# Edge counts and weight sums of a graph: blocks of 10 destinations in one PSUM bank, and each chunk's one-hots made once

## The reference

```python
N, C, E = (50000, 256, 9375)
msg = ew[:, None] * h[src]
agg = jax.ops.segment_sum(msg, dst, num_segments=x.shape[0])
```

```python
dst = jnp.concatenate([_d, _s, _loop])
_o = jnp.argsort(dst, stable=True)
dst = dst[_o]
```

## Time and profile before

| | us |
|---|---|
| median of three runs | 5758.88 |
| lowest and highest run | 5757.93, 5769.3 |
| span of the profiled execution | 5765.0 |
| of it `count_edges`: first to last instruction of its engines | 791.5 to 1649.2 |

### The profile page before, as it was taken

One profiled execution on the slowest core, in us unless ns is written; L12 is line 12 of the kernel. 1 busy time (PEld: TensorE's weight loads), 2 busy tenths in 40 slices (PEclk: granted clock), 3 DMA queues, 4 the chain that ended last, 5 costly groups with the idle time before them and its releaser, 6 DMA issues. The chain is left out here.

```text
span 5765.0 us, 88635 instructions
## 1 busy us (share of the span) xinstructions
PE 4607.2 (80%) x24482; PEld 3873.4 (67%) x24483; DVE 2716.3 (47%) x5068; ACT 2120.2 (37%) x3279; POOL 836.5 (15%) x769
## 2 busy tenths in 40 slices
PE   3888868888856499669589989899769959969666
PEld 2677645555545399438578778788659959969555
DVE  5555567777653400321379689689631140020233
ACT  2333215544433200424256566566524420020332
POOL 2778710000005200002100000000022200000000
PEclk8788889999968799789799999999779979989878
DMA  3433311211113342113211111111122134224000
GB/s 97 113 111 106 101 37 71 79 71 75 66 62 100 106 161 109 30 34 116 65 51 56 46 44 55 42 49 55 39 71 97 36 93 162 109 92 159 36 17 24
DMA packets 150165, 438.52 MB, mean 76 GB/s; under 512 B 25592, under 2 KB 89805, under 8 KB 133676
## 3 DMA queue, kind: packets, MB, share of 16 engines
q1 hardware_dynamic: 115212, 341.23, 16.7%
q0 software_dynamic: 34848, 96.08, 5.9%
HBM read 340.98 MB, written 96.25 MB: 76 GB/s over the span
## 5 line engine op out<-in xcount | busy, mean ns | idle before, releaser
L2404 PE MATMUL p_acc<-p_H,p_eT 125*125 125x256 f32 x3750 | 823.5, 378 | 0.0
L2404 PEld LDWEIGHTS p_acc<-p_H,p_eT 125*125 125x125 f32 x3750 | 695.2, 187 | 106.0
L1033 POOL DMA_INDIRECT p_message<-edge_table,p_index x425 | 503.8, 1185 | 131.2 <-issue 120.9
L1951 DVE TENSOR_REDUCE p_mean<-F 128x1 f32<-128x3125 f32 x10 | 34.0, 3403 | 931.7 <-PEq L83 931.7
L1246 PE MATMUL p_acc<-p_message,p_spread 125*125 125x260 f32 x1666 | 425.6, 422 | 28.7 <-issue 28.7
L1298 POOL IOTA p_order_i<- 125x200 int32 x3 | 1.1, 381 | 2882.6 <-SPq L81 2882.6
L1705 ACT ACTIVATE p_hid<-p_up,p_b1s 128x125 f32<-128x125 f32 x764 | 273.0, 366 | 395.6 <-PE p_up L1681 352.5
L1246 PEld LDWEIGHTS p_acc<-p_message,p_spread 125*125 125x125 f32 x1666 | 348.4, 211 | 98.1 <-issue 30.6
L1681 PEld LDWEIGHTS p_up<-p_xT,p_w1s 128*128 128x128 f32 x3056 | 377.8, 199 | 51.3 <-issue 33.1
L1681 PE MATMUL p_up<-p_xT,p_w1s 128*128 128x125 f32 x3056 | 385.5, 283 | 32.9 <-issue 11.8
L835 PE MATMUL p_acc<-p_cell,p_heavy 125*125 (+1 forms) x1440 | 405.4, 392 | 0.0
(11 more groups left out here) (441 smaller groups left out, 8080.0 us busy)
## 6 DMA issues: line engine op xcount, KB each, us to landing
sums_first<-edge_sums SPq DMA_DIRECT2D x48, 1250.0 KB
p_second<-edge_sums SPq DMA_DIRECT2D x48, 1250.0 KB, 6.7
p_count<-edge_counts SPq DMA_DIRECT2D x75, 762.9 KB
edge_sums<-p_sums SPq DMA_DIRECT2D x32, 1250.0 KB, 4.4
edge_counts<-p_total SPq DMA_DIRECT2D x32, 610.4 KB
p_w1s<-in_L_ffn_W SPq DMA_DIRECT2D x16, 1024.0 KB
p_got<-made SPq DMA_DIRECT2D x25, 560.0 KB
p_dst_all<-dst_row SPq DMA_DIRECT2D x25, 531.2 KB
```

Of the source, the lines that this page charges most:

```text
L1033: pool.indirect_dma_start(message[:, m, k, :], None, table, bass.IndirectOffsetOnAxis(ap=index[:, m, k:k + 1], axis=0)).then_inc(landed[m] ...
L1951: then(dve.tensor_reduce(mean[:, h:h + 1], F[:, h], AX_X, ALU.add))
L2404: last = pe.matmul(acc[:, s, 0:C], eT[:, r % 4, a % 4], H[:, a, 0:C], start=(a == 0), stop=(a == T - 1))
```

## The change

The block becomes 10 destinations and the group ten blocks, so a group still has 100 destinations, and the matrices in memory keep their shape. Counts and weight sums of a block share one PSUM bank (250 columns each), four banks in turn. The one-hots of a chunk (`lo` alone, and times three weight parts, now one instruction over 4 x 128 elements, with a part of ones in front) are made once, in a ring of four slots; a block whose first chunk was also the last of the block before uses the slot that is still there. `cell` is 250 wide, in a ring of four as well, counted by visits. Each block is one visit to the chunk before its first new one, and then a loop over `new` chunks; the loop has no separate lead. Because accumulation groups of two kinds share a bank, a last matmul with a zero operand of two columns closes the block.

ACT copies a block with one instruction, whose input is already in the order wanted. The transposes read `sums`, and are spread: four tiles after each of the first seven blocks. `total` and the semaphore of its stores have two turns. `load_graph` finds the chunks of 320 blocks instead of 160, and for each whether its first chunk was the last of the block before.

```diff
-BLK = 20
-TB = 5
+BLK = 10
+TB = 10
-LEAD = 3
+SETS_OF_BLOCKS = 4
+RING = 4
...
-            for m in range(2):
+            for m in range(SETS_OF_BLOCKS):
                 then(dve.tensor_scalar(below[:], ends_all[:, 0], start[:, m:m + 1], None, ALU.is_ge))
...
+            then(dve.tensor_scalar(q[:, 1, 0:n], q[:, 1, 0:n], 2.0, None, ALU.max))
+            then(dve.tensor_scalar(first, q[:, 0, 0:n], float(CH - 1), None, ALU.min))
+            then(dve.tensor_tensor(end, first, q[:, 1, 0:n], ALU.add))
+            then(dve.memset(again, 0.0))
+            then(dve.scalar_tensor_tensor(out=edge[:, 2, 1:n], in0=edge[:, 1, 0:n - 1], scalar=-1.0, in1=edge[:, 0, 1:n], op0=ALU.add, op1=ALU.is_equal))
+            then(dve.tensor_tensor(q[:, 2, 0:n], q[:, 1, 0:n], again, ALU.subtract))
+            then(dve.tensor_tensor(q[:, 0, 0:n], first, again, ALU.add))
...
+            def chunk(u, c):
+                dve.scalar_tensor_tensor(out=ring[:, turn_of(nc, u, RING)].rearrange("p a k n -> p (a k) n"),
+                                         in0=lane[:].unsqueeze(1).to_broadcast([P, KINDS, ROWS]), scalar=lo[:, chunk_at(nc, c)],
+                                         in1=part[:, :, chunk_at(nc, c)].to_broadcast([P, KINDS, ROWS]),
+                                         op0=ALU.is_equal, op1=ALU.mult).then_inc(chunk_ready, 1)
+            def cells(v, b, c):
+                dve.tensor_scalar(cell[:, turn_of(nc, v, RING)].rearrange("p a n -> p (a n)"), order[:], base[:, tile(b)],
+                                  key[:, chunk_at(nc, c)], ALU.add, ALU.is_equal).then_inc(cell_ready, 1)
             with dve.Fori(0, GROUPS) as j:
+                for s, (first, new, before) in enumerate(g.blocks_of(nc, DVE, j)):
                     b = j * TB + s
+                    v = before + b
+                    dve.wait_ge(visit_used, v + 1)
+                    cells(v, b, first)
+                    with dve.Fori(0, new) as i:
+                        dve.wait_ge(visit_used, v + i + 2)
+                        chunk(before + i, first + i)
+                        cells(v + i + 1, b, first + i + 1)
...
+            def add(at, v, u, start):
+                right = cell[:, turn_of(nc, v, RING)].rearrange("p a n -> p (a n)")
+                left = ring[:, turn_of(nc, u, RING)].rearrange("p a k n -> p (a k) n")
+                pe.matmul(at[:, 0:CELLS], left[:, 0], right, start=start, stop=False, skip_group_check=True)
                 for n in range(PARTS_OF):
+                    last = pe.matmul(at[:, CELLS:2 * CELLS], left[:, 1 + n], right, start=False, stop=False, skip_group_check=True)
+                last.then_inc(visit_used, 1)
...
+                at = acc[:, turn_of(nc, b, BANKS)].rearrange("p a n -> p (a n)")
                 pe.wait_ge(block_kept, b + 1)
+                pe.wait_ge(cell_ready, v + 1)
+                add(at, v, before + (RING - 1), True)
                 if block_of is not None:
                     loops(at, block_of)
+                with pe.Fori(0, new) as i:
+                    pe.wait_ge(chunk_ready, before + i + 1)
+                    pe.wait_ge(cell_ready, v + i + 2)
+                    add(at, v + i + 1, before + i, False)
+                pe.matmul(at[:, 0:2], zero16[:], zero16[:, 0:2], start=False, stop=True, skip_group_check=True).then_inc(block_summed, 1)
...
+                for s in range(TB):
+                    products(j + 1, s, own_blocks, None if looped is None else looped * TB + s)
+                    if s < len(FLIPS):
+                        turns(j, m, s)
...
+                act.wait_ge(block_summed, b + 1)
+                act.activation(sums[:, m, :, :, s * BLK:s * BLK + BLK],
+                               acc[:, turn_of(nc, b, BANKS), 0:2 * CELLS].rearrange("p a (k h d) -> p (a k) h d", k=2, h=T), ACT.Copy).then_inc(block_kept, 1)
```

More of the change, by code:

```diff
@@ L803, in cells @@
-            def cells(out, b, c):
-                dve.tensor_scalar(out, g.iota[:, 0:BLK * T], base[:, tile(b)], key[:, chunk_at(nc, c)], ALU.add, ALU.is_equal).then_inc(ready, 1)
+            then(dve.tensor_copy(lane[:], lane_i[:]))
+            dve.tensor_copy(order[:], order_i[:].rearrange("p h d -> p (h d)")).then_inc(setup, 1)
+            dve.wait_ge(setup, SETUP + 1)
+            dve.sem_inc(visit_used, RING)
+            dve.sem_inc(block_kept, BANKS)
+            dve.sem_inc(flip_kept, 4)
@@ L806, in _ @@
             with dve.Fori(0, GROUPS) as j:
-                for s, (first, rounds, before) in enumerate(g.blocks_of(nc, DVE, j)):
+                for s, (first, new, before) in enumerate(g.blocks_of(nc, DVE, j)):
                     b = j * TB + s
[L809 to L826, removed]
@@ L828, in _ @@
+                    v = before + b
[5 more added lines that the diff above has]
+                        cells(v + i + 1, b, first + i + 1)
         @block.tensor
         def _(pe):
-            pe.wait_ge(setup, SETUP)
-            def add(at, left, heavies, right, start=False, stop=False):
-                pe.matmul(at[:, 0, 0:BLK * T], left, right, start=start, stop=stop)
+            pe.wait_ge(setup, SETUP + 1)
@@ L842, in loops @@
                     if lo < hi:
-                        own = at[:, 0, 0:BLK * T].rearrange("p (d h) -> p d h", h=T)[:, lo - first:hi - first, t:t + 1].rearrange("p d h -> p (d h)")
-                        pe.matmul(own, ident16[:], ident16[:, lo - t * P:hi - t * P], start=False, stop=False)
+                        pe.matmul(at[:, t * BLK + lo - first:t * BLK + hi - first], ident16[:], ident16[:, lo - t * P:hi - t * P],
+                                  start=False, stop=False, skip_group_check=True)
@@ L846, in products @@
             def products(j, s, own_blocks, block_of=None):
                 b = j * TB + s
[L848 to L854, removed]
+                _, new, before = own_blocks[s]
@@ L861, in products @@
                     loops(at, block_of)
[L862 to L866, removed]
-                    pe.wait_ge(more_ready, before + i + 1)
-                    more = turn_of(nc, before + i)
-                    add(at, low_more[:, more].rearrange("p a n -> p (a n)"), heavy_more[:, more].rearrange("p a n m -> p (a n) m"),
-                        cell_more[:, more].rearrange("p a n -> p (a n)")).then_inc(more_used, 1)
@@ L871, in products @@
-                add(at, left[:, LEAD - 1], heavies[:, :, LEAD - 1], right[:, LEAD - 1], stop=True).then_inc(block_used, 1)
-            def turns(j):
-                pe.wait_ge(block_kept, (j + 1) * TB + 2)
-                for f, (a, e) in enumerate(FLIPS):
-                    pe.wait_ge(flip_kept, j * len(FLIPS) + f + 1)
-                    for h in range(a, e):
-                        last = pe.transpose(flip[:, f % 4, (h - a) * P:(h - a + 1) * P], turned[:, h], g.ident[0:P, 0:P])
-                    last.then_inc(flip_ready, 1)
@@ L891, in _ @@
             looped = -(-LOOPED // GD)
-            for j in range(looped - 1):
-                step(j, j + 1)
-            with pe.Fori(looped - 1, GROUPS - 1) as j:
-                step(j)
-            turns(GROUPS - 1)
+            ahead = looped - looped % 2
+            for j in range(ahead):
+                step(j, j % 2, j + 1 if j + 1 < looped else None)
+            with pe.Fori(ahead // 2, GROUPS // 2 - 1) as i:
+                step(i * 2, 0)
+                step(i * 2 + 1, 1)
+            step(GROUPS - 2, 0)
@@ L898, in _ @@
+            for f in range(len(FLIPS)):
+                turns(GROUPS - 1, 1, f)
         @block.scalar
         def _(act):
[L900 to L910 removed]
```

176 lines of the change are left out of this document (93 added, 83 removed).

## The result

The changed kernel takes 6153.34 us (6152.01 to 6158.67) against 5758.41 beside it: a ratio of 1.069 [1.067, 1.070]. 6200 was predicted, in a range of 6010 to 6410.

What follows compares the result with a forecast made beforehand. PE's instruction queue was taken as the bound: 39.4 us a group instead of 26.05, 427 us more over 32 groups, plus 12 in `load_graph` and 4 for self-loop matmuls, 443 in all, gave 6200 us, range 6010 to 6410.

Steps and rivals of the forecast that it cites:

- The bound: `count_edges`: PE's queue instructions set the pace, 3.7 us a block before, at full and fallen clock alike.
- Blocks: PE's queue in `count_edges`: 3.0 us per block after (2.6 to 3.9), 30.0 a group where 18.5 stood.
- The register load: PE's queue, per group: eleven registers 2.1 us (1.15 to 3.0); with 0.45 between and 2.8 for pairs, 5.35.
- The transposes: PE's queue, per group: spread over seven blocks with two waits each, they stay 3.6 us (2.8 to 4.2).
- The sum: A group on PE's queue: 30.0 + 5.35 + 3.6 = 39.0 us, 39.4 with the carried remainder.
- the 0.45 carried over: Per group: half of the 0.95 us left unexplained before (branch back, slow start after the load), added to 39.0.
- `load_graph`: The stage ahead: DVE's serial chain and four more transposes cost 12 us more (8 to 16).
- the opening of the stage: First groups of `count_edges`: thirty more self-loop matmuls at 0.15, 4 us; set-up before them 0 (-2 to 3).
- What hides: Work beside PE's queue, per group: DVE 25 us, array 13 to 26, ACT 10 to 15, all covered by 39.
- A queue that could run ahead: Rival 1, `count_edges`: array and DVE set the pace, 22 us a group, 5645 us in all; chance 0.09.
- A visible load of DVE: Rival 2: with the ring, DVE's and PE's register loads stand in sequence, up to 171 us more, 6370; chance 0.10.
- no change: Rival 3: loop trips and block heads get cheaper, a block 1.7 and a group 26 us, 5765; chance 0.03.

Runs made afterwards that it cites:

- the run with five buffers: Kernel before with constant buffers and PSUM banks, records of eight numbers, and the leads' one-hots in five buffers instead of two: 5608.81 us, 0.974.
- the change with blocks of 20: The changed kernel with five blocks of 20 destinations a group, two PSUM banks each, instead of ten of 10: 5802.2 us, 1.007 of the kernel before.

## Why the prediction was right, point by point

**The bound.** PE's queue sets the pace after as before. Shown from three sides: two register operations more per trip cost 115 us, though their matmuls add only 1760 columns to 0.76 million; a load shortened on the queue by 73 us returns 76; a longer ring, more DVE work and fewer columns return or cost 10 us at most. The array is less far off than the text had it (below), but not the bound.

**Blocks.** 3.0 us were predicted for the mean. 200 of one trip at 2.5 and 120 of two at 3.9 [queue rows above] give (200 x 2.5 + 120 x 3.9) / 320 = 3.0: 30 a group, as forecast.

**The register load.** Predicted 2.1, by six registers' mean times 11 / 6; measured 3.62. The rows of before held the warning: 0.82 to 1.48 for one and the same load, which I averaged instead of asking what alternates. From the load's end at 1408.5 to the next block's opening at 1411.8 are 3.3 us, as predicted (0.45 + 2.8). The load itself lay outside the range given (1.15 to 3.0). So 6.9 a group where 5.35 were forecast: 50 us too little over 32 groups.

**The transposes.** Predicted 3.6 a group on the queue (2.8 to 4.2); they cost about 1: that is what the sum below leaves, and in the trace a block followed by one of the seven turns is 0.1 us longer than one that isn't. A later turn of four, by the queue's rows: its second wait (L884) starts at 1418.4, the next block's opening at 1418.5. Their addresses are constants, so no register operation stands between them; the 2.83 us of the earlier trace rows were the array's time, which now lies beside the queue's. Over 32 groups some 80 us too much.

```profile
L884 PEldq ALU_OP  x1: 39/39/39, 1418.4 to 1418.4; - x1
...
L870 PEldq ALU_OP  x1: 32/32/32, 1418.5 to 1418.5; - x1
```

**The sum.** 30 + 6.9 + 1 = 37.9, and 38.00 measured; 39.4 was forecast. Two of its terms were outside their own ranges, with errors of opposite sign (1.6 too little, 2.6 too much), and the 0.45 carried over was not needed: the path and the blocks were right by reasoning, that the sum came so close is in part luck. `load_graph` 10.6 against 12, the opening of the stage 5.0 against 4. In all 395 against the 441 that separate 6200 from the runs of before.

**What hides.** DVE's instructions were sized 0.69 and 0.30 and took 0.75 and 0.345; its waits for visits are 349.5 + 65.6 = 415 us, 13 a group, as said. Wrong in size were three signs: the load (above), the granted clock, 0.74 and not near 0.5, and PE busy 63% of the stage, not well under half. Half of the columns do not halve the busy time: a matmul of 250 columns takes 0.28 us at full clock and 0.39 to 0.42 at half, where one of 500 took 0.374. One reading was wrong without effect: DVE had eight instructions a block before (1275 by 160), not seven, so its limit was lower still.

```profile
L852 PE MATMUL p_acc<-p_cell,p_ring x760: 267/278/415, 818.2 to 2023.5; 125*128 x190
```

**The rivals.** A queue that could run ahead (5645) is not seen: the array waits 282 us on "issue". Where register operations are taken off the queue, as in the run with five buffers, matmuls of 500 columns do follow each other every 0.21 us for whole blocks: 28 of them between the two rows below. The Trainium skill, TensorE: Matmul & The Clock Gate, Back-to-back issue gap, gives 0.211 by the formula that the prediction quoted; it holds where the queue keeps up, and not in this change. A visible load of DVE (6370) fell with the longer ring, and no change (5765) with the result.

```profile
1200.02 0.38 PE L842 MATMUL p_acc<-p_cell,p_low 125*125 125x500 bf16 x1
...
1205.92 0.37 PE L842 MATMUL p_acc<-p_cell,p_low 125*125 125x500 bf16 x1
```

## What to carry to other kernels

A matmul whose address comes from a register cost the queue about 0.13 us here, with 2 columns as with 250, so cutting tiles smaller to save columns makes a kernel slower once the queue is the bound: look whether the pace is the same at full and at half clock. Take the register operations out (unroll until buffers and banks are constants) and make the buffers deep enough to cover the producer's own loads in the same step, as either alone shows little. Ask of every row with two durations what alternates.

## What the runs showed of the hardware

- How long a load of registers takes depends on where its record starts, and on more. Eleven registers took PE's queue 1.33 us from a multiple of 16 bytes and 3.9 to 4.7 us otherwise. DVE's took 1.31, and otherwise 2.5 to 2.9 with four slots in the ring and up to 4.9 with eight (first two rows below). Six took 0.82 or 1.47 us in the kernel before, and 0.82 each time from records of 32 bytes, but from the same records up to 2.83 on PE and 3.65 on DVE in the change with blocks of 20 (last two rows). What lengthens them there stays open.
- The Trainium skill, Runtime: NRT & Kernel Launch, Instruction fetch mechanics, puts loads of registers at about 200 ns per register; those it speaks of come from HBM. Here, from a record in SBUF, PE's took 0.12 to 0.14 us per register where they were short, and up to 0.43 in the changed kernel's long ones.

```profile
L171 DVEq TENSOR_LOAD <-block_chunks x32: 1306/2518/2936, 812.5 to 1978.0; - x32
...
L171 DVEq TENSOR_LOAD <-block_chunks x32: 1306/4454/4920, 809.9 to 1969.0; - x32
...
L171 PEldq TENSOR_LOAD <-block_chunks x32: 835/1470/2830, 798.9 to 1653.0; - x32
L171 DVEq TENSOR_LOAD <-block_chunks x32: 814/1562/3651, 799.4 to 1649.5; - x32
```

- Four pairs of weight load and matmul with constant addresses passed PE's queue within some 0.1 us; two with register operations cost 0.27.
- Half the columns in the loop's matmuls made the granted clock fall from 0.74 to 0.55, and the array's busy time rose from 773 to 803 us.
